# Turning a second attention tile of every four by DMA, and working out V's scale an image later

## The reference

```python
# layer 0: attention of x with itself
S   = softmax(einsum('bcn,bcm->bnm', Wb @ x, Wc @ x))
x   = gamma * einsum('bcm,bnm->bcn', Wd @ x, S) + x
# layer 1: group norm, then attention in 4 heads of 64 channels
hn  = group_norm(x, 32 groups) * gamma + beta
q, k, v = wq @ hn + bq, wk @ hn + bk, wv @ hn + bv
a   = softmax(einsum('bhdq,bhdk->bhqk', q, k) * 64 ** -0.5)
out = x + wp @ einsum('bhqk,bhdk->bhdq', a, v) + bp
```

## Time and profile before

| what | value |
| --- | --- |
| median of 3 runs (lowest, highest) | 688.39 us (685.99 to 689.23) |
| the profiled execution's own time | 689.51 us |
| its span, first to last instruction | 687.8 us |
| PE, PEld, DVE, ACT, POOL busy | 95%, 73%, 77%, 66%, 44% |
| bytes moved by DMA | 85.75 MB |

### The profile page before, as it was taken

One profiled execution on the slowest core, in us unless ns is written; L12 is line 12 of the kernel. 1 busy time (PEld: TensorE's weight loads), 2 busy tenths in 40 slices (PEclk: granted clock), 3 DMA queues, 4 the chain that ended last, 5 costly groups with the idle time before them and its releaser, 6 DMA issues.

```text
span 687.8 us, 10563 instructions
## 1 busy us (share of the span) xinstructions
PE 652.4 (95%) x3424; PEld 499.0 (73%) x3424; DVE 529.5 (77%) x857; ACT 455.8 (66%) x759; POOL 305.2 (44%) x259
## 2 busy tenths in 40 slices
PE   8969999999999799889989999999999999999997
PEld 7857788888888687666667766676876766776665
DVE  5767677776778638698878888877888878888886
ACT  5444344335443418789867889877889877878885
POOL 0260111112115105587554668655478645556641
PEclk9988999999999989999999999999999999999999
DMA  7445757565583767641398724387923457732321
GB/s 230 92 87 129 155 121 136 143 150 107 139 182 79 163 172 163 128 81 44 85 200 183 177 47 107 77 176 168 223 46 82 100 127 177 174 76 77 62 61 62
DMA packets 161210, 85.75 MB, mean 125 GB/s; under 512 B 135568, under 2 KB 137872, under 8 KB 161168
## 3 DMA queue, kind: packets, MB, share of 16 engines
q1 hardware_dynamic: 161168, 85.23, 54.7%
HBM read 18.62 MB, written 8.39 MB: 39 GB/s over the span
## 4 chain that ended last, share of the span: by engine, by line
PE 55%; ACT 14%; issue 8%; POOL 7%; DVE 7%; SPq 4%; DMA 3%; POOLq 0%; DVEq 0%; ACTq 0%
PE acc L1604 23%; PE scores L1604 17%; PE trans L1604 8%; PE trans L1638 6%; ACT prob L873 4%; SPq L553 3%; ACT pt L894 3%; DVE negmax L1135 3%; ACT prob_more L873 3%; POOL planes L734 2%; POOL prob L727 1%; ACT o_sum L1058 1%; DMA y_in<-y_scratch 1%; ACT planes L906 1%; POOL planes L772 1%
## 5 line engine op out<-in xcount | busy, mean ns | idle before, releaser
L1135 DVE TENSOR_REDUCE negmax<-scores 128x1 f32<-128x1024 f32 x160 | 194.0, 1213 | 15.1 <-PE scores L1604 13.2
L1604 PE MATMUL scores<-k_st,q_st 128*128 128x512 f32 x512 | 162.0, 438 | 4.0 <-issue 2.3
L873 ACT ACTIVATE prob<-scores,negmax 128x1024 f32<-128x1024 f32 x96 | 107.3, 1117 | 86.8 <-DVE negmax L1135 85.6
L727 POOL TENSOR_SCALAR prob<-prob,rsum 128x1024 f32<-128x1024 f32 x64 | 72.0, 1125 | 152.0 <-DVE rsum L1141 152.0
L1604 PE MATMUL acc<-pt,v_st 128*128 128x512 f16 (+1 forms) x528 | 131.8, 374 | 4.7 <-DVE pt L1159 1.9
L894 ACT ACTIVATE pt<-trans 128x512 f16<-128x512 f32 x194 | 105.1, 593 | 37.6 <-PE trans L1638 37.2
L1159 DVE TENSOR_TENSOR pt<-trans,pt 128x512 f16<-128x512 f32 x194 | 124.0, 681 | 0.4 <-ACT pt L894 0.4
L1604 PEld LDWEIGHTS scores<-k_st,q_st 128*128 128x128 f32 x512 | 96.0, 189 | 34.6 <-issue 3.2
L772 POOL TENSOR_SCALAR planes<-prob,rsum 128x1024 f16<-128x1024 f32 x32 | 36.7, 1148 | 165.3 <-DVE rsum L1141 161.9
L1604 PEld LDWEIGHTS acc<-pt,v_st 128*128 128x128 f16 x528 | 44.5, 98 | 59.8 <-issue 16.9
L873 ACT ACTIVATE prob_more<-scores,negmax 128x1024 f32<-128x1024 f32 x64 | 71.5, 1117 | 17.6 <-DVE negmax L1135 17.3
(11 more groups left out here) (189 smaller groups left out, 1186.0 us busy)
## 6 DMA issues: line engine op xcount, KB each, us to landing
k_st<-qk SPq DMA_DIRECT2D x64, 256.0 KB, 4.7
q_st<-qk SPq DMA_DIRECT2D x64, 128.0 KB, 2.3
x_raw<-in_x SPq DMA_DIRECT2D x8, 512.0 KB, 5.2
y_out<-in_x SPq DMA_DIRECT2D x16, 256.0 KB, 3.3
y_scratch<-y_out SPq DMA_DIRECT2D x16, 256.0 KB, 2.2
y_in<-y_scratch SPq DMA_DIRECT2D x4, 1024.0 KB, 7.6
y_res<-y_scratch SPq DMA_DIRECT2D x16, 256.0 KB, 3.8
out<-y_res SPq DMA_DIRECT2D x14, 256.0 KB, 2.8
```

The source lines that it names most:

```text
L727: nc.gpsimd.tensor_scalar(prob1(t), prob1(t), rsum[:, t % 4:t % 4 + 1], PROB_SCALE, ALU.mult, ALU.mult)\
L873: nc.scalar.activation(dst, scores[:, t % 2, :], ACT.Exp, bias=negmax[:, t % 2:t % 2 + 1], scale=1.0, accum_out=rowsum[:, column:column + ...
L1135: nc.vector.tensor_reduce(negmax[:, t % 2:t % 2 + 1], scores[:, t % 2, :], AX_X, ALU.max, negate=True).then_inc(max_ready, 1)
L1604: ins = nc.tensor.matmul(dst, w, m, start=(starts and n == 0), stop=(stops and n == len(pairs) - 1))
```

## The change

In layer 1 the tile with s % 4 == 1 is turned by DMA too: ACT makes its high plane as it does for s % 4 == 0, DVE its low plane (the tile in f32 minus the high plane, into f16), and SP issues one more 512 KB transpose for every four tiles. PE, ACT and DVE no longer transpose and evacuate it through PSUM. `load_y` moves from s == 3 to s == 2 in the first image and to s == 0 in the others, ahead of the second transpose and of `qk7`'s restack.

V's bound and scale get a buffer of their own, `v_work`. `value_factors` moves behind image 0's last tile on POOL. PE's `vb`, the power, the reciprocal, the picks, the scaling and the high and low part of `wv` move to the last image of layer 0. The picks and the scaling of `wv` go from DVE to POOL. The 1 / V_SPAN of the scale is folded into the first instruction.

```diff
-PARTS0_FIRST = ["d0", "d1", "d2", "d3", "vb", "av0", "av1", "next_a0", "next_a1", "next_a2", "next_a3"]
+PARTS0_FIRST = ["d0", "d1", "d2", "d3", "av0", "av1", "next_a0", "next_a1", "next_a2", "next_a3"]
-PARTS0_LAST = [("prev_av2", 0, 2), ("prev_av2", 1, 2), "prev_av3", "d0", "d1", "gn0", "gn1", "d2", "d3",
+PARTS0_LAST = [("prev_av2", 0, 2), ("prev_av2", 1, 2), "prev_av3", "d0", "d1", "vb", "gn0", "gn1", "d2", "d3",
...
-TURNED = (0,)
+TURNED = (0,1,)
-LOW_ON_VECTOR = ()
+LOW_ON_VECTOR = (1,)
...
+        v_work = sb("v_work", [P, KT, 2, H])
...
@@ SP, image1(i) @@
-                    if s == 3 and not plan.last:
+                    if s == (2 if plan.first else 0) and not plan.last:
                         sp.wait_ge(h_split, 4 * i + 4)
                         load_y(i + 1)
...
@@ POOL @@
             for t in range(T0_IMAGE):
                 high_plane(0, t)
-                if t == 4:
-                    value_factors()
+            value_factors()
...
-            for t in range(5, T0_IMAGE):
+            high_plane(IMAGES - 1, 5)
+            pool.wait_ge(v_chain, 1)
+            for k in range(KT):
+                cols = slice(k * P, (k + 1) * P)
+                nc.gpsimd.tensor_tensor(v_picked[:, cols], v_power[:, cols], ident[:, :], ALU.mult).then_inc(v_picks, 1)
+            pool.wait_ge(v_chain, 2)
+            for k in range(KT):
+                nc.gpsimd.tensor_tensor(wv_raw[:, k, :], wv_raw[:, k, :], v_scale, ALU.mult).then_inc(v_scaled, 1)
+            for t in range(6, T0_IMAGE):
                 high_plane(IMAGES - 1, t)
...
@@ ACT, image 0 @@
             turned_high(0, 7)
-            act.wait_ge(v_scaled, KT)
-            nc.scalar.activation(w_hi["v"][:, :, :], wv_raw, ACT.Copy).then_inc(wv_high, 1)
...
@@ ACT, image IMAGES - 1 @@
             exp0(IMAGES - 1, 7)
+            act.wait_ge(v_scaled, KT)
+            nc.scalar.activation(w_hi["v"][:, :, :], wv_raw, ACT.Copy).then_inc(wv_high, 1)
...
@@ DVE @@
-            def value_scales():
+            def value_power(plan):
+                wait_acc(plan.number("vb"))
+                nc.vector.tensor_scalar(v_limit, group_out(plan, "vb", slice(0, C)), V_LEAST, 1.0 / V_SPAN,
+                                        ALU.max, ALU.mult).then_inc(acc_evac, 1)
...
+            def value_scale():
                 dve.wait_ge(v_chain, 1)
                 nc.vector.reciprocal(v_scale, v_power).then_inc(v_chain, 1)
...
+            def value_unscale():
+                dve.wait_ge(v_picks, KT)
...
+            def value_weight_low():
                 dve.wait_ge(wv_high, 1)
...
                 turned_low(0, t)
-            value_scales()
...
             turned_low(e, 3)
+            value_power(last_plan)
             norm_deviations(0, last_plan)
             norm_variance(0, last_plan)
             max0(e, 4)
             norm_affine(0)
             norm_next(0)
+            value_scale()
             recip0(e, 4)
             d_low(e, 2)
...
             recip0(e, 6)
+            value_unscale()
             max0(e, 7)
...
             stats(e, 3)
+            value_weight_low()
...
@@ PE, image 0 @@
-            pe.wait_ge(v_factors, 10 + KT)
-            group(plan0(0), "vb", [(v_spread[:, k, :], wv_size[:, k, :]) for k in range(KT)], slice(0, C))
             d_split(0)
             values0(0, "av0")
...
@@ PE, image IMAGES - 1 @@
             first_half(e)
+            pe.wait_ge(v_factors, 10 + KT)
+            group(last_plan, "vb", [(v_spread[:, k, :], wv_size[:, k, :]) for k in range(KT)], slice(0, C))
             pe.wait_ge(gn_stats, KT * GN_SETS[0][1])
```

More of the change, by code:

```diff
@@ L122 @@
 FOUR_BANKS = ("first_a", "layer0_first", "layer0")
-FOUR_BANKS_LAST = ("prev_av2", "prev_av3", "d0", "d1", "gn0", "gn1", "d2", "d3", "av0", "next_qk0", "next_qk1", "av1")
+FOUR_BANKS_LAST = ("prev_av2", "prev_av3", "d0", "d1", "vb", "gn0", "gn1", "d2", "d3", "av0", "next_qk0", "next_qk1", "av1")
 def place_groups():
@@ L439, in build @@
         v_scaled = sem("v_scaled")
+        v_picks = sem("v_picks")
         wv_high = sem("wv_high")
@@ L498, in slot_free @@
             return plan1(i).number("prev_av7") if j == 1 else plan1(i).base - (LAYER1[::-1].index("av6") + 1)
[L502 to L505, removed]
+        wv_raw, wv_size = v_work[:, :, 0, 0:C], v_work[:, :, 0, C:2 * C]
+        wv_least = v_work[:, :, 1, C:2 * C]
+        v_spread = v_work[:, :, 1, 0:P]
+        v_limit, v_power = v_work[:, 0, 1, C:2 * C], v_work[:, 1, 1, C:2 * C]
+        v_scale, v_picked = v_work[:, 0, 1, 0:C], v_work[:, 1, 1, 0:C]
         def d_part(buf, n):
@@ L1329, in turned_low @@
                                         None, ALU.mult).then_inc(pt_split, 1)
-            def value_scales():
[L1334 to L1337, removed]
+            def value_power(plan):
+                wait_acc(plan.number("vb"))
+                nc.vector.tensor_scalar(v_limit, group_out(plan, "vb", slice(0, C)), V_LEAST, 1.0 / V_SPAN,
+                                        ALU.max, ALU.mult).then_inc(acc_evac, 1)
+                dve.wait_ge(acc_evac, EVAC_CREDIT + plan.number("vb") + 1)
                 nc.vector.tensor_scalar(v_power.bitcast(mybir.dt.int32), v_limit.bitcast(mybir.dt.int32),
                                         0x7F800000, None, ALU.bitwise_and).then_inc(v_chain, 1)
+            def value_scale():
                 dve.wait_ge(v_chain, 1)
                 nc.vector.reciprocal(v_scale, v_power).then_inc(v_chain, 1)
[L1342 to L1346, removed]
+            def value_unscale():
+                dve.wait_ge(v_picks, KT)
                 nc.vector.tensor_reduce(v_bound[:, 0, :], v_picked.rearrange("p (k c) -> p k c", c=P), AX_X, ALU.add)\
                     .then_inc(v_chain, 1)
[L1349 to L1353, removed]
+                dve.wait_ge(v_chain, 3)
+                nc.vector.tensor_scalar(v_unscale[:, :], v_bound[:, 0, :], 1.0 / PROB_SCALE, None, ALU.mult)\
                     .then_inc(v_chain, 1)
+            def value_weight_low():
                 dve.wait_ge(wv_high, 1)
```

## The result

The changed kernel takes 714.4 us (712.5 to 714.8, 4 runs), against 688.8 (686.0 to 690.5) before: a ratio of 1.037, interval 1.034 to 1.039. The forecast was 702.0 with a range up to 714. The sign was right; the loss is 25.6 us where 13.6 were forecast. Most of what the forecast named is there, at the places that it named, but the term of SP's queue was far too small.

What follows compares the result with a forecast made beforehand. Two loops of nearly equal length, PE's work and the DVE-ACT chain, were taken to bind each other. Terms -10.7 + 3.2 - 1.5 + 5.5 + 17.1 = +13.6 us gave 702.0 us at the median, range 678 to 714.

Steps and rivals of the forecast that it cites:

- the term of SP's queue: Layer 1's image starts and ends: added transfers and earlier load_y delay restacks that PE's scores need; +17.1 us (0 to 24).
- the shares as they were charged: Queue delay charged: 4.5 of 7.0 us in image 0, two thirds at the next two starts, one tile at each end.
- a rival at 0.10: Longer PE stands at image starts drop the clock to 0.5, up to 3.6 us each; 710 to 716 us, chance 0.10.
- tiles 25 and 29 ahead of the restacks of `qk4` to `qk6`: Image ends: two transposes put 4.66 us more into SP's queue; one tile, 2.33, charged at three ends, +7.0 us.
- tile 8's scores waiting for `qk7`'s restack: Starts of images 1 and 2: 7.0 us added against 2.85 of slack, two thirds of the lateness taken, +2.8 us each.
- the sign that was named: PE waiting over 2 us for `k_st` at tile 8 of each image shows the queue term; no such wait refutes it.
- PE is not the bound: Layer 1: 31.9 us of PE transposes leave, only -1.5 us returns; rival with PE the bound 655 to 678 us, chance 0.10.
- VectorE beside GpSimd: Layer 1: DVE's new low plane, with two SBUF inputs, is slowed beside POOL operations; +5.5 us (-2 to 9).
- V's scale: Layer 0: leaving image 0 gives -10.7 us (-8 to -11.5); arriving in the last image costs +3.2 (2 to 5).
- only as a bound: Layer 0, image 0: the gain is only -8 us if PE still has a wait that lets the clock fall.

Runs made afterwards that it cites:

- experiment 3: Kernel before with load_y moved as in the change and 31 further 512 KB transposes that nothing reads; 720.2 us, ratio 1.047.
- experiment 4: Changed kernel with the second tile's DMA transpose cut to one sixteenth for 29 of its 31 tiles; 702.0 us, ratio 1.020.
- experiment 2: Changed kernel with load_y back at s == 3, behind the second transpose and qk7's restack; 707.9 us, ratio 1.027.
- experiment 5: As experiment 4, with VectorE's low plane of that tile also cut to 64 of its 1024 columns; 693.5 us, ratio 1.007.

## Why the prediction was right or wrong

**Wrong: the queue's term, and in it first the price of a transpose.** The prediction took 2.33 us for a tile, from 512 KB at the 225 GB/s of the earlier trace rows. That is a mixed rate, of restacks, loads and two of the kernel's own transposes. The changed kernel's page gives the price itself: 66.4% of 713.0 less 54.7% of 687.8 is 97.2 us for 31 tiles, 3.14 each, and experiment 3 has 3.21. The rate of one kind of transfer was used for another: a transposed 512 KB is 2080 packets, where a copy of the same size is 144. The trace of before held the kind already. By its packet records the 63 times 512 KB that it transposes in both layers keep the 16 engines busy for 181.1 us, 2.87 each.

**Wrong: nothing in the sum for the clock behind these stalls.** With 3.14 in place of 2.33 and the shares as they were charged, the term would have been 4.5 / 7.0 x 7.8 = 5.0 us at the start of image 0, 2 x 2/3 x 4.95 = 6.6 at the next two and 3 x 3.14 = 9.4 at the ends, 21 us in all, and the forecast 706. Measured are 27.2. Behind the stands PE's scores start 6.5 us later than before at the start of image 0, 3.9 and 3.4 at the next two, and 2.5, 2.7 and 2.3 at the ends (each less the difference that the tile ahead already had): 21.3 us. So the shares came out about right in sum, in part by luck, for image 0 lost more and the ends less. The other 6 us pass behind these starts, at a granted clock of 0.50. At the end of image 1 the 2.7 became 5.3; at the end of image 2, where the clock stayed at 1.00 behind a stand of 2.98 us, nothing was added to the 2.3. The prediction had this as a rival at 0.10, with three stalls of 3.6 us and 710 to 716 us, where the measured time lies; there were five, of 0.4 to 2.5 us each. Price and clock together, 4 and 6 us, are what the forecast lacked.

**Right places, wrong readers.** At the ends the prediction had tiles 25 and 29 ahead of the restacks of `qk4` to `qk6` and charged one of the two. PE's first wait there is for `qk2` and `qk3`, and only tile 25 is ahead of those. At the starts of images 1 and 2 it had tile 8's scores waiting for `qk7`'s restack. PE waits earlier, at 392.88, for tile 1's own transpose, which stands behind `load_y`; the restack is late as well, as experiment 3 shows, but hidden behind that. So the sign that was named, a wait of over 2 us for `k_st` at tile 8 of each image, is missing in two images, and would have refuted a term that was there. Cutting the transpose took 6.7 of these 8.3 us off (experiment 4), and moving `load_y` back 6.3 (experiment 2), of which 3.9 came back behind them.

**Right: PE is not the bound.** For 31.9 us of PE work 1.5 were booked. With most of the transfers and the low plane out of the way the steps give back 1.4, and none is under the old beat (experiment 5). The Trainium skill, "Trainium Kernel Development and Optimization" (opening part, "Reading a trace"), calls matmul busy a bad metric and weight-load busy a good one. The runs agree: of the 31.9 us taken from an engine that was 95% busy, some 30 gave nothing.

**Right: VectorE beside GpSimd.** +5.5 and -1.5 were booked and 4.3 measured; with the 1.4 of experiment 5 that makes 5.7 for the low plane. Its group and GpSimd's normalisation in the changed kernel:

```profile
L1163 DVE TENSOR_TENSOR planes<-prob,planes 128x1024 f16<-128x1024 f32 x31 | 49.4, 1594 | 2.2 <-ACT planes L916 2.2
...
L786 POOL TENSOR_SCALAR y_in<-y_in,gn_now 128x512 f32<-128x512 f32 x16 | 21.9, 1371 | 6.6 <-DMA y_in<-y_scratch 6.6
```

A low plane takes 1.59 us on average, 0.38 over the 1.21 of a lone one, which is 11.9 us for 31; about half of it stands on the path. Of the 31, 29 began while a GpSimd instruction ran, and each of these took the rest of that instruction and 1.07 to 1.08 us more. At 434.78 the rest was 434.51 + 1.12 - 434.78 = 0.85, and the low plane took 1.92; the two evacuations that it replaces take 1.28 together in that step of the kernel before. The other two met no GpSimd instruction and took 1.21 and 1.22:

```profile
396.82 1.21 DVE L1163 TENSOR_TENSOR planes<-prob,planes 128x1024 f16<-128x1024 f32 x1
```

In experiment 5 the narrow low planes take the same rest and 0.07 to 0.08 us: 0.92 at 429.35, with 0.85 left. The Trainium skill, "SBUF — State Buffer" ("SBUF: two separate sides"), has each of the two engines lock the other out for the whole of an instruction. The trace agrees: the whole rest passes first. Against a lone one, which takes 0.14 us more than 1.07, the loss is that much less than the rest, 0.71 of 0.85 here and 0.29 of 0.42 in the row that I had used.

**Right: V's scale**, -9.2 + 3.0 against -10.7 + 3.2. The clock still falls behind a PE wait of 1.87 us, which the prediction kept only as a bound; in the runs where it did not fall, image 0 gave 10.8 to 10.9 us.

**What stays open.** Whether a transfer's price counts by the busy time of the DMA engines or by the time that it holds SP is not separated. Nor is it shown why the clock falls behind some of PE's stands and not behind others of the same length.

## What to carry to other kernels

A transfer is to be priced in busy time for its own kind, never in bytes at another kind's rate: here transposing 512 KB cost 3.1 to 3.2 us, copying it 1.4. Where a queue is full, find in SP's order the first reader behind what is put in: here one transpose ahead of it made PE's stand 2.7 to 3.1 us longer. Where a stall on PE is forecast, the sum needs a term for the clock behind it, here up to 2.5 us each. Moving work off an engine that is 95% busy gains little (here 1.4 of 31.9 us) while another loop has the same beat. When a change bundles two parts, run them apart: here one was worth 7.8 us and the other cost over 30.

## What the runs showed of the hardware that I had not expected

A plain copy of 512 KB within SBUF keeps the 16 DMA engines busy for only 1.39 us, less than the 2.33 of the mixed traffic's rate. GpSimd suffers beside VectorE's low planes too. Its normalisation of 128x512 takes 1.37 us on average, with 1.73 in the row at 435.62, where the group of the kernel before had 0.886; with the narrow low planes of experiment 5 it is back at 0.880:

```profile
L783 POOL TENSOR_SCALAR y_in<-y_in,gn_now 128x512 f32<-128x512 f32 x16 | 14.1, 886 | 9.4 <-DMA y_in<-y_scratch 9.4
```

The clock is not the same from run to run. Behind one and the same stand of PE in image 0 of layer 0, 1.86 to 1.87 us long, it fell to 0.50 in three runs and stayed at 1.00 in three, and that is worth 1.6 us (9.2 against 10.8).
